# The first two row tiles of a graph aggregation by plain fp32 matmuls, with x split behind them and loaded ahead of the second tile

## The reference

```python
def _L0_gnn_ref(cur, incidence_m):          # cur = x (4096 x 256), incidence_m = adj (4096 x 4096)
    mask = incidence_m > 0
    head = mask.astype(incidence_m.dtype)
    head = head / jnp.maximum(jnp.sqrt(jnp.sum(head * head, axis=-1, keepdims=True)), EPS)
    inc = incidence_m + head
    edge_fea = inc @ cur
    edge_degree = jnp.sum(inc, axis=-1, keepdims=True)
    return edge_fea / edge_degree

def reference(x, adj):
    return _layernorm(x + _L0_gnn_ref(x, adj), axis=-1)
```

## Time and profile before

| | |
|---|---|
| median of three runs | 436.32 us (435.46 to 437.48) |
| the profiled execution | 437.03 us, of which the span is 435.2 us |
| PE, DVE, POOL, ACT busy | 90%, 85%, 85%, 80% |
| DMA | 79.8 MB, 183 GB/s over the span |
| granted PE clock, mean | 0.98 |

### The profile page before, as it was taken

The page is one execution under the profiler, slowest core; times in us unless marked ns, Lnnn a source line. Parts: engine busy times, 40 slices in busy tenths (PEclk is TensorE's granted clock), DMA queues, the critical chain, the costliest instruction groups (busy, mean ns, idle before and its releaser), DMA issues.

```text
span 435.2 us, 8833 instructions
## 1 busy us (share of the span) xinstructions
PE 392.1 (90%) x2148; PEld 343.6 (79%) x2148; DVE 368.6 (85%) x739; ACT 347.8 (80%) x452; POOL 369.4 (85%) x274
## 2 busy tenths in 40 slices
PE   0056479999999999999999999999999999999995
PEld 0036368888888888888888888888888888888884
DVE  0436788999999999999999999999999999999932
ACT  4655899889888998988998888898889988886200
POOL 1096878999999999999999999999999999999860
PEclk9996789999999999999999999999999999999999
DMA  7999575566667766666666666666666666670010
GB/s 198 218 265 256 172 221 184 174 197 191 191 208 207 217 195 196 192 193 194 195 194 193 199 202 217 206 185 207 189 194 193 192 195 196 199 213 24 24 39 12
DMA packets 38090, 79.84 MB, mean 183 GB/s; under 512 B 9408, under 2 KB 21696, under 8 KB 38080
## 3 DMA queue, kind: packets, MB, share of 16 engines
q1 hardware_dynamic: 38080, 79.73, 63.0%
HBM read 75.50 MB, written 4.19 MB: 183 GB/s over the span
## 4 chain that ended last, share of the span: by engine, by line
PE 84%; SPq 5%; issue 5%; DMA 3%; DVE 2%; ACT 0%; POOLq 0%; POOL 0%; ACTq 0%; DVEq 0%
PE edge L584 42%; PE edge L587 22%; PE edge L558 19%; DMA rows<-in_x_dram 3%; SPq L152 3%; SPq L171 1%; PE sums L545 1%; DVE inc L412 1%; DVE incT L422 1%; SPq L168 1%; SPq L175 0%; ACT scaled L218 0%; POOLq L46 0%; POOL rstd L315 0%; DVE rows L449 0%
## 5 line engine op out<-in xcount | busy, mean ns | idle before, releaser
L584 PE MATMUL edge<-x_split,inc_hi 128*128 128x512 f32 (+1 forms) x864 | 304.4, 399 | 4.1 <-POOL x_split L369 2.7
L330 POOL TENSOR_TENSOR inc_lo<-incT,inc_hi 128x832 fp32r<-128x832 f32 x126 | 248.7, 1985 | 12.1 <-DVE incT L422 7.7
L587 PE MATMUL edge<-x_split,inc_lo 128*128 128x256 f32 x832 | 235.8, 283 | 0.0
L584 PEld LDWEIGHTS edge<-x_split,inc_hi 128*128 128x128 f32 x864 | 165.0, 191 | 40.6 <-POOL x_split L369 3.0
L209 ACT ACTIVATE sign_out<-raw,sign_bias 128x1024 bf16<-128x1024 f32 x128 | 146.4, 1144 | 35.4 <-DMA raw<-in_adj_dram 33.9
L412 DVE SCALAR_TENSOR_TENSOR inc<-raw,scaled 128x1024 f32<-128x1024 f32 x128 | 153.6, 1202 | 9.3 <-ACT scaled L218 9.3
L587 PEld LDWEIGHTS edge<-x_split,inc_lo 128*128 128x128 f32 x832 | 160.1, 192 | 0.0
L422 DVE STREAM_TRANSPOSE incT<-inc 128x1024 f32<-128x1024 f32 x128 | 155.4, 1227 | 0.0
L218 ACT ACTIVATE scaled<-raw,norm 128x1024 f32<-128x1024 f32 x128 | 141.6, 1108 | 9.7 <-DVE inc L412 5.3
L558 PE MATMUL edge<-x_native,incT 128*128 128x256 f32 x384 | 97.5, 394 | 11.9 <-DMA x_native<-in_x_dram 11.9
L558 PEld LDWEIGHTS edge<-x_native,incT 128*128 128x128 f32 x384 | 69.9, 194 | 20.7 <-DVE incT L422 12.0
(11 more groups left out here) (30 smaller groups left out, 86.6 us busy)
## 6 DMA issues: line engine op xcount, KB each, us to landing
raw<-in_adj_dram SPq DMA_DIRECT2D x512, 128.0 KB, 2.6
rows<-in_x_dram SPq DMA_DIRECT2D x32, 128.0 KB, 2.1
out_dram<-rows SPq DMA_DIRECT2D x32, 128.0 KB, 1.8
incT<-in_x_dram SPq DMA_DIRECT2D x4, 512.0 KB, 9.9
rows<-in_x_dram SPq DMA_DIRECT2D x4, 320.0 KB, 12.3
x_native<-in_x_dram SPq DMA_DIRECT2D x4, 192.0 KB, 10.8
```

The costliest lines, as they stand in the source:

```text
L330: nc.gpsimd.tensor_tensor(inc_lo[:, s, :, q, :], incT[:, s, 0:SPLIT, q, :], hi_of(s, q).bitcast(fp32), ALU.subtract).then_inc(lo_by_pool, ...
L584: nc.tensor.matmul(edge[s][:, c0:c1], inc_hi[:, s, b, :, :].rearrange("p q j -> p (q j)"), x_split[:, b, :, :].rearrange("p h d -> p (h d) ...
L587: last = nc.tensor.matmul(edge[s][:, D:2 * D], inc_lo[:, s, b, :, :].rearrange("p q j -> p (q j)"), x_split[:, b, 0, :], start=False, stop ...
```

## The change

Tiles 0 and 1 are multiplied without any split: all 32 blocks as plain fp32 matmuls, with x as it was loaded (`native_tile`). x is loaded whole into a buffer `x_stage` that shares its memory with slot 1 of the split `inc` (the two buffers `inc_hi` and `inc_lo` become `inc_split0` and `inc_split1`, one per slot). x is split in four parts behind the preparation of tile 1: ACT rounds all four, POOL subtracts two, DVE two. The split product begins with tile 2. Tile 0's count and norm are made quarter by quarter (`sum_first`, `first_count_of`, and POOL's four powers of 128 x 1). The DMAs of tile 0 are issued half by SP (groups 0, 1) and half by ACT (groups 2, 3). After them come the 6 plain blocks, the 26 others in 16 DMAs, group order 0, 2, 1, 3, then `raw` of tile 1.

```diff
+            for k in range(G):
+                for g in (0, 1):
+                    load_piece(sp, 0, 0, k, g)
+            for g in PORT_ORDER:
                 sp.dma_start(x_native[SQ * g:SQ * (g + 1), :, :], x_v[g, :, SPLIT:B, :]).then_inc(x_native_in, 16)
+            for c in range(4):
+                for g in PORT_ORDER:
+                    sp.dma_start(x_stage[SQ * g:SQ * (g + 1), X_AT[c]:X_AT[c + 1], :],
+                                 x_v[g, :, X_AT[c]:X_AT[c + 1], :]).then_inc(x_in[c], 16)
             for k in range(G):
                 load_quarter(1, 1, k, False)
...
+            def native_matmul(s, b, x_of_b, start, stop):
+                return nc.tensor.matmul(edge[s][:, 0:D], incT[:, s, b, :, :].rearrange("p q j -> p (q j)"), x_of_b,
+                                        start=start, stop=stop)
+
+            def native_tile(t, s, middle):
+
+                pe.wait_ge(incT_ready, G * t + G)
+                if t == 0:
+                    pe.wait_ge(x_native_in, FOUR_DMAS)
+                for n in range(NATIVE):
+                    if n in middle:
+                        middle[n]()
+                    native_matmul(s, SPLIT + n, x_native[:, n, :], n == 0, False)
+                for b in range(SPLIT):
+                    if t == 0 and b in X_AT:
+                        pe.wait_ge(x_in[X_AT.index(b)], FOUR_DMAS)
+                    if NATIVE + b in middle:
+                        middle[NATIVE + b]()
+                    last = native_matmul(s, b, x_stage[:, b, :], False, b == SPLIT - 1)
+                return last
...
             pe.wait_ge(consts_ready, 1)
-            sum_signs(0, 0)
...
+            for q in range(G):
+                sum_first(q)
+            native_tile(0, 0, {3: lambda: sum_signs(1, 1)}).then_inc(edge_ready, 1)
+            native_tile(1, 1, {12: lambda: sum_quadrants(0, 0, reuse=False, first=True),
+                               26: lambda: sum_quadrants(1, 1, reuse=False)}).then_inc(edge_ready, 1)
+            tile(2, 0, first=True)
+            tile(3, 1)
+            with pe.Fori(2, PAIRS - 1) as u:
...
             for q in range(G):
                 sign_quarter(1, 1, 0, q, reuse=False)
+            for q in range(G):
+                scale_quarter(1, 1, q)
+            for c in range(4):
+                split_x_hi(c)
+
+            for q in range(G):
+                sign_quarter(2, 0, 1, q, reuse=False)
+            scale_quarter(2, 0, 0)
+            scale_quarter(2, 0, 1)
             sign_quarter(3, 1, 1, 0)
             sign_quarter(3, 1, 1, 1)
+            tile(2, 0, 1, reuse=False)
...
             norm_of(1, 1)
...
+            for c in X_LO_POOL:
+                split_x_lo(c)
+            norm_of(2, 0)
+            tile(2, 0, reuse=False)
```

More of the change, by code:

```diff
@@ new lines, in _ @@
+            act.wait_ge(consts_ready, 1)
+            nc.scalar.activation(table_load[:, :], sign_bias[:, :], ACT.Sign)
+            sign_quarter(0, 0, 0, 0, first=True, reuse=False)
+            sign_quarter(0, 0, 0, 1, reuse=False)
+            scale_quarter(0, 0, 0, first=True)
+            sign_quarter(0, 0, 0, 2, reuse=False)
+            scale_quarter(0, 0, 1, first=True)
+            sign_quarter(0, 0, 0, 3, reuse=False)
+            scale_quarter(0, 0, 2, first=True)
+            scale_quarter(0, 0, 3, first=True)
@@ L285, in _ @@
+            tile(3, 1, 1, staged=True)
+            with act.Fori(2, PAIRS - 1) as u:
                 tile(2 * u, 0, u)
@@ new lines, in _ @@
+            transpose_quarter(0, 0, 2, False, False)
+            inc_quarter(0, 0, 3, False, False)
+            transpose_quarter(0, 0, 3, False, False)
+            count_of(1, 1)
+            for q in range(G):
+                inc_quarter(1, 1, q, True, False)
+                transpose_quarter(1, 1, q, False, False)
+            for c in X_LO_DVE:
+                split_x_lo(c)
+            count_of(2, 0)
+            tile(2, 0, 1, native=True, slot_split=False, norm_before=False)
+            tile(3, 1, 1, native=True, slot_split=False, reuse_result=False)
@@ L528, in _, with sum_first @@
         def _(pe):
+            def sum_first(q):
+                pe.wait_ge(signs_ready, q + 1)
+                nc.tensor.matmul(first_sums[q][:, 0:1], quad_sum[:, :], part_sums[:, 0, 1, q:q + 1],
+                                 start=True, stop=True).then_inc(first_summed, 1)
             def sum_signs(t, s):
@@ new lines, in native_tile, with native_products, split_products @@
+                return last
+            def native_products(t, s, signs):
+                pe.wait_ge(incT_ready, G * t + G)
+                pe.wait_ge(y_ready, t - 1)
+                for n in range(NATIVE):
+                    last = native_matmul(s, SPLIT + n, x_native[:, n, :], n == 0, False)
+                    if n == SUMS_AT:
+                        sum_quadrants(t, s, signs=signs)
+                last.then_inc(native_done, 1)
+            def split_products(t, s, first):
+                pe.wait_ge(lo_by_pool, G * (t - FIRST_SPLIT) + G)
+                if first:
+                    pe.wait_ge(x_lo_by_pool, len(X_LO_POOL))
+                    pe.wait_ge(x_lo_by_dve, len(X_LO_DVE))
+                for b in range(SPLIT):
@@ L604, in _, with tile @@
-            tile(0, 0, reuse=False, first=True)
-            tile(1, 1, reuse=False)
-            with pe.Fori(1, PAIRS - 1) as u:
+                last.then_inc(edge_ready, 1)
+            SUMS_AT = 3
+            def tile(t, s, signs=True, first=False):
+                native_products(t, s, signs)
+                split_products(t, s, first)
+            pe.wait_ge(consts_ready, 1)
+            for q in range(G):
+                sum_first(q)
+            native_tile(0, 0, {3: lambda: sum_signs(1, 1)}).then_inc(edge_ready, 1)
```

326 lines of the change are left out of this document (135 added, 191 removed).

## The result

The changed kernel took 443.24 us (median of 4 runs, 442.76 to 445.42), the kernel before 435.89 us (the three runs given above and a fourth, 434.44 to 437.48): ratio 1.0154, 95% interval 1.0128 to 1.0179. It is slower by 1.5%. The forecast was 442.0 us with the range 437.0 to 447.5. The profiled execution took 442.76 us, its span 440.9 us, which is 5.7 us over the span of before (435.2 us); the sum of the prediction had 5.6.

A forecast was written before the change was run, and what follows sets the result against it. PE bounds the kernel: a start of some 72 us, then 30 tiles at its pace. Tile 2's split 3.9 us later plus 1.7 for restart makes 5.6, so 442.6 us profiled, median 442.0, range 437.0 to 447.5.

The forecast's parts named there:

- Another pace of the matmuls: Rival: buffers laid out anew make both slots run like the faster or slower one, 2.2 us gained or lost; chance 0.10.
- The sum of tile 1's signs: PE's sum waiting for tile 1's last quarter, now behind all of x: from 34.52 to 35.8 us, +2.7 and -1.4.
- the second queue: Tile 0's load issued from two queues: 7.3 us at best instead of 8.7, taken as -1.4 us.
- The sum that gives tile 2's count: PE's sum behind 41 plain products counted from tile 1's sum of signs: 56.5 us, where it was 51.33.
- Cost 0, at worst 1: POOL's and DVE's low parts of x ahead of tile 2's norm: just in time, 0 us added, at worst 1.
- PE's 41 products: Plain products between tile 1's sum of signs and the sum for tile 2's count: 17.7 us at full clock.
- The chain from there: From the sum for tile 2's count: 10.1 us to the next sum (66.6), 12.1 to POOL's last low quarter (78.7).
- The restart: PE enters tile 2's split products after three waits at a lower clock: 1.7 us lost, bounds 0 and 2.8.
- the four marks: Start of the kernel: tile 1's sum at 35.8, tile 2's at 56.5, the next at 66.6, first split at 78.8 us.
- Fast x with a warm PE: Rival: x loads at 287 GB/s and PE loses nothing at tile 2 after its waits, 436.8 us; chance 0.15.
- Slow x: Rival: 1 KB rows limit x to 215 GB/s and two queues bring nothing, 446.8 us; chance 0.15.
- Faster: Rival: tile 1 lands so early (sum at 28.0 us) that PE's extra work fits its old waits; chance 0.07.

The follow-up runs named there:

- the run with both edits: Changed kernel with x's split moved ahead of tile 1's signs, and those signs summed behind 24 products of tile 0 instead of 3: 443.86 us, ratio 1.0162.
- the first edit: Changed kernel with tile 1's raw loaded ahead of the 26 staged blocks of x instead of behind: 432.6 us, ratio 0.9897; again 433.76 us, 0.9949.
- the later group: Changed kernel run again unedited, 443.35 us, beside the kernel before, 437.63 us: ratio 1.0137.
- the old order with the small pieces: Changed kernel with the 16 DMAs of staged x in group order 0, 1, 2, 3 instead of 0, 2, 1, 3: 444.45 us, ratio 1.0145.
- the sum behind product 24: Changed kernel with PE summing tile 1's signs behind 24 products of tile 0 instead of 3: 443.19 us, ratio 1.0137.

## Why the prediction was right

- **The shape.** "A start of some 72 us and then 30 tiles at PE's pace", with the pace untouched: 11.92 us per tile after, 11.91 before. Another pace of the matmuls didn't come.
- **The sum of tile 1's signs**, 35.8 us by the sum, was at 37.35. Two terms were off. x came at 236 GB/s and not at 260, which in the prediction's own formula is 4.19/0.236 = 17.8 us, +4.4 instead of +2.7; and the second queue gave about 0.2, in the one pair of traces, instead of 1.4. With both, 34.52 + 4.4 - 0.2 = 38.7, and tile 1 at 270 instead of 287 GB/s would add another 0.5; the trace has 37.35 and other executions 36.06 to 38.49. So with the measured rates the sum comes out more than 1 us too large: something else in it errs the other way, no run shows what, and it hid part of the two errors. The mechanism (all of x now ahead of tile 1) is the one that putting tile 1 first undid.
- **The sum that gives tile 2's count**: +20.7 predicted, +19.8 measured, 57.14 against 56.5. The 29 products at the head took 51.96 - 37.80 = 14.16 us, 1.6 over their 12.5 at full clock; I had 2.8. Of these the first three took 40.49 - 37.80 = 2.69 us for 1.30. The profile's granted clock says 1.00 there; the clock records of this trace begin only at 41 us, so the loss is seen in the products alone. "Cost 0, at worst 1" for POOL and DVE was right in size and named the wrong engine: POOL's norm waited for DVE. The text had DVE's low parts run beside POOL's and, for the worst case, added their 2 x 1.7 us to POOL's, 20.5 in all. The worst case came: the four ran as if one after the other and ended 20.7 behind the sum of tile 1's signs, with DVE last. The count came at 57.99, some 0.5 later than behind the sum alone.
- **PE's 41 products as what fills this step** is the weakest link of the text. They were one of four ways within 1.7 us of each other (PE 19.8, DVE's low parts 20.7, tile 1's transposes and 12 products 20.25 in the run with both edits, ACT 19.0, for which the text had 18.7); with 21 of the products gone nothing moved. The number was right and the reason only part of it.
- **The chain from there**: 10.1 to the next sum, measured 67.52 - 57.14 = 10.4, of which 0.5 is DVE. From the count it is 9.5 us in the changed kernel (57.99 to 67.52) and in the first edit (46.63 to 56.17). The 12.1 to the split was 79.46 - 67.52 = 11.9. Split at 79.46, 4.5 later than before where 3.9 were summed.
- **The restart**: 1.7 predicted. On the chain it is 90.08 - 79.46 = 10.6 us from tile 2's first split product to tile 3's plain products, and was 84.48 - 74.95 = 9.5: 1.1. On PE's timeline, whose rows begin 0.16 earlier than the chain's, it is 10.5, and against an execution at full clock (9.1) 1.3 more.
- **The sum**: 4.5 + 1.1 = 5.6, predicted 3.9 + 1.7 = 5.6. Each of the four marks came 0.6 to 1.6 us late, the restart 0.6 short. These errors cancel, and that the sum is met to 0.1 us is luck; that it is met to 1 or 2 is not. The medians differ by 443.24 - 435.89 = 7.4 us; in the later group by 5.7 (443.35 and 437.63). The forecast of 442.0 thus lies 1.2 low, less than the two medians' own spread.
- **The rivals.** Fast x with a warm PE (436.8) fell with the 236 GB/s. Slow x (446.8) fell too: x came at 236 and not at 215. The rule on ports (the Trainium skill, SBUF — State Buffer, section on the DMA port swizzle) says that partitions 0 to 63 reach only eight of the sixteen ports. The prediction drew from it that x could go at the rate of `raw` in the new order. `raw` went at 270 in the same trace and x at 236, and the old order with the small pieces had 223, so the order alone doesn't give the rate of these loads, and why x stays below `raw` wasn't tried. "Faster" needed the sum of tile 1's signs at 28.0; with tile 1 loaded first it comes at 23.05, and the kernel is faster than before by 1.0% and, in its second group, 0.5%, so the point at which it decides was on the right side.

## What to carry to other kernels

Work taken off a start that waits for loads is worth nothing if the bytes it needs are put ahead of the bytes that the chain waits for: follow the one load whose arrival releases everything (here tile 1's last quarter), and keep it where it was, before counting what the engines save. Where moving one engine's share changes nothing, look for ways of equal length from the same releaser rather than conclude that the releaser is wrong; two edits that each did nothing, and nothing together, pointed to it here. And an operation filled into a wait costs what it costs beside its neighbours, not alone: DVE's and POOL's subtractions took here as long as one after the other.

## What the runs showed of the hardware beyond expectation

- Two subtractions by DVE (128x1536) and two by POOL (128x1792), put side by side, took 11.1 us together in the changed kernel. Alone they take 1.76 us each and 3.96 each, 11.4 in all. Each operation that began while the other engine's was running took longer by about what the other still had to do: DVE's first 2.48 (0.9 left of POOL's first), POOL's second 5.51 (1.7 left of DVE's first), DVE's second 5.54 (3.9 left of POOL's second).
- The same load list landed at times that differ by 2.4 us (36.06 to 38.49 for the sum of tile 1's signs).
- The granted clock behind a wait differs between executions of nearly the same list: from 78 to 82 us it was 0.57 and 0.77 in two traces of the changed kernel and 1.00 with the sum behind product 24. The stretch from tile 2's first split product to tile 3 took 10.5, 10.7 and 9.1 us, so the cost at that place was 0 to 1.6 us.
